# Attention maxima as three bfloat16 parts for a bfloat16 selector product, in a four-layer cross-attention kernel

## What is computed

```python
scores = jnp.einsum('bshd,bmhd->bhsm', qh, kh) / jnp.sqrt(hd)
probs = jax.nn.softmax(scores, axis=-1)
mem_out = jnp.einsum('bhsm,bmhd->bshd', probs, vh).reshape(B, S, D) @ Awo + abo
```

## Time and profile before

| what | us |
|---|---|
| median of three runs | 1187.8 (1187.23 to 1188.69) |
| time of the profiled execution | 1181.47 |
| its span, first to last instruction | 1179.7 |
| TensorE busy (matmul) | 981.0, 83% of the span |
| VectorE busy | 596.5, 51% |
| ScalarE busy | 428.1, 36% |
| mean granted TensorE clock | 0.873 of full |

### The profile page before, as it was taken

One profiled execution on the slowest core, in us unless ns is written; L12 is line 12 of the kernel. 1 busy time (PEld: TensorE's weight loads), 2 busy tenths in 40 slices (PEclk: granted clock), 3 DMA queues, 4 the chain that ended last, 5 costly groups with the idle time before them and its releaser, 6 DMA issues.

```text
span 1179.7 us, 11621 instructions
## 1 busy us (share of the span) xinstructions
PE 981.0 (83%) x4601; PEld 453.8 (38%) x4604; DVE 596.5 (51%) x881; ACT 428.1 (36%) x557; POOL 43.3 (4%) x42
## 2 busy tenths in 40 slices
PE   4867799669899899677799899895888798886877
PEld 2323244243344234253221443632346444542332
DVE  3238999972203210636821423516849774964342
ACT  3442222334322432363133143345572166123534
POOL 0000000200000000200000000000002000100000
PEclk9988899868998989776588789698989898987999
DMA  7000000000000000200000000000000000000000
GB/s 304 1 0 0 0 1 0 0 1 1 0 1 1 1 1 0 101 0 12 4 0 1 1 1 1 2 1 1 13 1 1 1 0 1 1 1 0 1 36 36
DMA packets 3526, 15.49 MB, mean 13 GB/s; under 512 B 933, under 2 KB 1445, under 8 KB 2842
## 3 DMA queue, kind: packets, MB, share of 16 engines
q1 hardware_dynamic: 3338, 12.77, 2.9%
q0 software_dynamic: 144, 2.10, 0.4%
HBM read 11.92 MB, written 2.10 MB: 12 GB/s over the span
## 4 chain that ended last, share of the span: by engine, by line
PE 57%; DVE 23%; ACT 9%; issue 8%; DMA 1%; SPq 1%; DVEq 0%; POOLq 0%; POOL 0%; ACTq 0%
PE ps L362 56%; DVE AR L1391 3%; DVE AR L1392 2%; ACT AR L572 2%; DVE AR L1544 2%; DVE AR L1689 1%; DVE VB L583 1%; DVE AR L461 1%; DVE AR L1394 1%; DVE AR L1676 1%; ACT AR L440 1%; DVE AR L1680 1%; DMA X<-in_xT 1%; DVE AR L1685 1%; ACT AR L445 1%
## 5 line engine op out<-in xcount | busy, mean ns | idle before, releaser
L362 PE MATMUL ps<-AR,WA 128*128 128x512 f32 (+3 forms) x808 | 365.8, 616 | 25.4 <-DVE AR L461 6.1
L362 PEld LDWEIGHTS ps<-AR,WA 128*128 128x128 f32 (+2 forms) x808 | 154.9, 197 | 230.6 <-issue 198.7
L362 PE MATMUL ps<-AR,CN 128*128 128x512 f32 (+3 forms) x350 | 147.1, 660 | 48.5 <-DVE AR L458 32.4
L362 PE MATMUL ps<-AR 128*64 128x128 f32 (+6 forms) x592 | 125.0, 373 | 11.1 <-DVE AR L1678 5.9
L362 PEld LDWEIGHTS ps<-AR,CN 128*128 128x128 f32 (+2 forms) x350 | 49.3, 175 | 116.0 <-issue 70.8
L591 DVE TENSOR_TENSOR AR<-ps,AR 128x512 f32<-128x512 f32 x24 | 16.6, 691 | 120.2 <-ACT AR L577 120.2
L583 DVE TENSOR_REDUCE VB<-ps 128x16 f32<-128x1232 f32 x32 | 45.3, 1440 | 46.2 <-PE ps L362 46.2
L362 PEld LDWEIGHTS ps<-AR 128*64 128x64 f32 (+5 forms) x592 | 49.8, 148 | 48.1 <-issue 22.9
L572 ACT ACTIVATE AR<-ps 77x2048 f32<-77x2048 f32 x24 | 44.1, 1870 | 61.4 <-PE ps L362 61.4
L1155 ACT ACTIVATE AR<-ps 128x512 f32<-128x512 f32 x48 | 28.7, 597 | 97.4 <-DVE AR L1394 49.9
L1468 DVE SCALAR_TENSOR_TENSOR X<-ps,VC,X 128x512 f32 x8 | 5.6, 747 | 106.7 <-PE ps L362 106.7
(11 more groups left out here) (271 smaller groups left out, 1133.9 us busy)
## 6 DMA issues: line engine op xcount, KB each, us to landing
WA<-in_m SPq DMA_DIRECT2D x1, 2856.0 KB, 9.1
WA<-in_m SPq DMA_DIRECT2D x1, 2560.0 KB, 14.3
X<-in_xT POOLq DMA_DIRECT2D x1, 2048.0 KB, 9.0
WA<-in_m SPq DMA_DIRECT2D x1, 2048.0 KB, 19.5
out<-X SPq DMA_DIRECT2D x4, 512.0 KB, 3.1
WB<-in_m SPq DMA_DIRECT2D x1, 1028.0 KB, 21.4
WA<-in_m SPq DMA_DIRECT2D x1, 512.0 KB, 15.1
VB<-AR SPq DMA_DIRECT2D x12, 32.0 KB, 1.8
```

What stands on the lines that cost most here:

```text
L362: return nc.tensor.matmul(out, lhsT, rhs, start=first, stop=last)
```

## The change

Each negated maximum m is written as three parts. `high` is m rounded to bfloat16, the remainder is formed in float32, rounded to bfloat16 again, and what is left is the third part. They lie in columns i, 4 + i and 8 + i of the head's 32 in `MXP[b]`, still a float32 tile, so that after the transposes they stand on three partitions. VectorE does this for each batch with six linked operations right after the batch's last maximum, 16 values for each set and partition at a time (32 in a0 and a3, 64 in a2), and counts up `att_ms`, for which the transposes of the batch now wait. The copy out of the accumulator writes `MXT[b]` in bfloat16. `sel` has ones in rows i, 4 + i and 8 + i, and is copied once, at the start, to the bfloat16 tile `SELB`. The selector product is one bfloat16 product for each head in place of a float32 one.

```diff
--- before.py
+++ after.py
@@ -84,7 +84,7 @@
         part = np.float32(np.trunc(rest / unit) * unit)
         c[k::32, CONST["neg"][0]] = part
         rest = np.float32(rest - part)
-    put("sel", p[:, None] % 32 == np.arange(4))
+    put("sel", (p[:, None] % 32 < 12) & (p[:, None] % 4 == np.arange(4)))
     put("half", (p[:, None] // 16 % 2 == np.arange(2)) * 16 ** -0.5)
     put("den", (p == 5)[:, None] * np.ones(6))
     put("head", p[:, None] % 32 == np.arange(HM))
@@ -253,7 +253,8 @@
         PF = [[a[:, 6 * T + k * ROWC * P:6 * T + (k + 1) * ROWC * P] for k in range(2)] for a in PX]
         PTX = [a[0:M, 0:8 * T].rearrange("m (s r t) -> m s r t", s=2, r=4) for a in PX]
         MXP = [VB[:, b * 1024:b * 1024 + T].rearrange("p (s n) -> p s n", s=SUB) for b in range(B)]
-        MXT = [VB[:, b * 1024 + T:b * 1024 + 2 * T] for b in range(B)]
+        MXT = [VB[:, b * 1024 + T:b * 1024 + T + T // 2].bitcast(BF16) for b in range(B)]
+        MXH = [VB[:, b * 1024 + T + T // 2:b * 1024 + T + T // 2 + 2 * SUB * 4].bitcast(BF16).rearrange("p (s r n) -> p s r n", s=SUB, r=4) for b in range(B)]
         PR = [[PF[b][k][:, 0:SLOTS * M].rearrange("p (h m) -> p h m", h=SLOTS) for k in range(2)] for b in range(B)]
         XC = [c3.take(DC, T) for _ in range(B)]
         RTB = [c3.take(T) for _ in range(B)]
@@ -333,6 +334,7 @@
         KEEP = sb("KEEP", [P, M])
         NEG3 = sb("NEG3", [P, HALF], BF16)
         ONESB = sb("ONESB", [P, P], BF16)
+        SELB = sb("SELB", [P, 4], BF16)
 
         class Chain:
 
@@ -531,7 +533,7 @@
                             last = mm(bank(b, r)[:, s * M:(s + 1) * M], QS[b][row, g, s * P:(s + 1) * P], KF[row, k, g, b, :], not masked, s == SUB - 1 or not masked)
                     last.then_inc(sem("att_p1"), 1)
             for b in BS:
-                pe.wait_ge(*after("att_mx", nset(p, j, len(sets) - 1, b)))
+                pe.wait_ge(*after("att_ms", nunit(p, j, b)))
                 for s in range(SUB):
                     last = nc.tensor.transpose(bank(b, 0)[:, s * P:(s + 1) * P], MXP[b][:, s, :], cn("ident"))
                 last.then_inc(sem("att_mt"), 1)
@@ -550,7 +552,7 @@
                             mm(bank(b, r)[0:M, :], KF[row, k, g, b, :], QS[b][row, g, :], True, False)
                         for r in range(4):
                             row = slice(32 * r, 32 * r + 32)
-                            last = mm(bank(b, r)[0:M, :], cn("sel")[row, i:i + 1].broadcast_to([32, M]), MXT[b][row, :], False, True)
+                            last = mm(bank(b, r)[0:M, :], SELB[row, i:i + 1].broadcast_to([32, M]), MXT[b][row, :], False, True)
                         last.then_inc(sem("att_p2"), 1)
                 for b in BS:
                     pe.wait_ge(*after("att_ex", nset(p, j, sets.index((g, PARTS[p] - 1)), b)))
@@ -576,12 +578,25 @@
                     act.wait_ge(*after("att_ln", nchunk(p, j, g, b)))
                     nc.scalar.activation(RTB[b], RTB[b], ACT.Exp, scale=-1.0).then_inc(sem("att_r"), 1)
 
-        def attn_dve(dve, p, j):
+        def attn_dve(dve, ch, p, j):
             for i, (g, k) in enumerate(key_sets(p)):
                 for b in BS:
                     dve.wait_ge(*after("att_p1", nset(p, j, i, b)))
                     nc.vector.tensor_reduce(MXP[b].rearrange("p s (r n) -> p r s n", n=32)[:, :, :, i],
                                             ps[:, 4 * b:4 * b + 4, 0:HALF].rearrange("p r (s m) -> p r s m", m=M), AX.X, ALU.max, negate=True).then_inc(sem("att_mx"), 1)
+                    if i < DC * PARTS[p] - 1:
+                        continue
+                    sets = DC * PARTS[p]
+                    parts = [MXP[b].rearrange("p s (r n) -> p s r n", n=32)[:, :, :, 4 * k:4 * k + sets] for k in range(3)]
+                    high = MXH[b][:, :, :, 0:sets]
+                    dve.wait_ge(*after("att_mx", nset(p, j, i, b)))
+                    for k in range(2):
+                        ch.link(nc.vector.tensor_copy(high, parts[k]))
+                        ch.link(nc.vector.tensor_tensor(parts[k + 1], parts[k], high, ALU.subtract))
+                        ins = nc.vector.tensor_copy(parts[k], high)
+                        if k == 0:
+                            ch.link(ins)
+                    ins.then_inc(sem("att_ms"), 1)
             for b in BS:
                 dve.wait_ge(*after("att_mt", nunit(p, j, b)))
                 nc.vector.tensor_copy(MXT[b], bank(b, 0)).then_inc(sem("att_mc"), 1)
@@ -1336,6 +1351,7 @@
             dve.wait_ge(*after("ld_vec", 16))
             dve.wait_ge(*after("ld_x", 16))
             dve.wait_ge(*after("ld_cn", 16))
+            nc.vector.tensor_copy(SELB[:, :], cn("sel"))
             norm_dve(dve, "r1", 0, lambda q: X[:, :, part_of(q)[0], part_of(q)[1]], RTR1, lambda q: XN[:, :, part_of(q)[0], part_of(q)[1]], False, None, SQR1,
                      UNITS, lambda q, k: ps[:, q, :])
             dve.wait_ge(*after("ld_w0", 16))
@@ -1450,7 +1466,7 @@
             dve.wait_ge(*after("mz", 1))
             with dve.Fori(0, J) as j:
                 ch.enter(j)
-                attn_dve(dve, "a0", j)
+                attn_dve(dve, ch, "a0", j)
                 for b in BS:
                     for mo in range(DC):
                         xd = X[:, mo, b, tj(j)]
@@ -1597,7 +1613,7 @@
             dve.wait_ge(*after("mz", 2))
             with dve.Fori(0, J) as j:
                 ch.enter(j)
-                attn_dve(dve, "a2", j)
+                attn_dve(dve, ch, "a2", j)
                 for b in BS:
                     for mo in range(DC):
                         xd = X[:, mo, b, tj(j)]
@@ -1703,7 +1719,7 @@
             with dve.Fori(0, J) as j:
                 ch.enter(j)
                 norm_dve(dve, "l3", j, lambda b: xs(b, j), RTB, lambda b: XC[b], True, XC, ST)
-                attn_dve(dve, "a3", j)
+                attn_dve(dve, ch, "a3", j)
                 for b in BS:
                     for mo in range(DC):
                         xd = X[:, mo, b, tj(j)]
```

## The result

| what | before | after |
|---|---|---|
| median of the runs, us | 1184.16 (20 runs beside it, 1181.91 to 1189.83) | 1191.65 (20 runs, 1186.67 to 1199.70) |
| ratio to before, 95% interval | | 1.0059 (1.0042 to 1.0077) |
| span of the profiled execution, us | 1179.7 | 1186.9 |
| mean granted TensorE clock | 0.873 | 0.859 |

A forecast was written before the change was run, and what follows sets the result against it. A sequence of handovers, no full engine, bounds the kernel (TensorE 57% of the chain, VectorE 23%). Delays of 16.7 us less savings gave +5.7, with layer 3's clock +6.7, on the median 1187.8: 1194.5 us, range 1190 to 1199.

The forecast's parts named there:

- the clock of layer 3: Layer 3: clock may fall before the second scores, costing 1.6 us a unit; a third taken, 0.5 each.
- Split, 1.36 and 1.56 us: Six linked VectorE operations per batch ahead of its transposes: 1.36 us in layers 0 and 3, 1.56 in layer 2.
- Delay of the second scores, 16.7: Second scores start two splits later: 2.56 us twice (layer 0), 2.96 twice (layer 2), 2.82 twice (layer 3).
- First product: A unit's first selector product (batch 0) counts whole: gains 1.54, 1.30, 1.40, 0.79 us, and 0.67 in layer 3.
- What ScalarE hides: Batch 1's first product is hidden behind batch 0's exponential, ScalarE taking 1.87 us a batch; not every saving counts.
- the second chunk's: In every unit's second chunk, one product between a batch's att_ctx and its exponential is on the path: 0.67 us gained.
- the small slacks: Waits of ScalarE that faster products remove: 0.27 us in the first unit, 0.29 in layer 2's second half.
- third rival: Clock falls in both layer 3 units and rises later in layers 0 and 2: +12.5, 1200.3 us; chance 0.19.
- A (-7.4): Selector's full saving lands in all 32 pairs of second scores: 24.1 us against 16.7 of delay, 1180.4; chance 0.08.
- B (no change): Clock has risen when layers 0 and 2's later second scores start: +1.3, 1189.1 us, no measurable change; chance 0.11.
- D (+15): The bfloat16 selector products run in turn, no faster than float32 ones: some +15, 1203 us; chance 0.04.
- the signs named beforehand: Profile after: 128 bfloat16 selector records, splits 1.3 to 1.6 us, back-to-back exponentials, half clock in layer 3's first scores.

The follow-up runs named there:

- e2: Changed kernel without the split: each maximum rounded to one bfloat16 part, bfloat16 selector product kept; ratio to before 0.9910.
- e3: Changed kernel with six more linked operations of the same shapes ahead of each split, into a spare tile; ratio to before 1.0233.
- e1: Changed kernel with the split kept but the selector product and its copy back in float32; ratio to before 1.0198.
- e4: Changed kernel with unread mask products (9 and 14) on TensorE while layer 3's splits run; ratio to before 1.0022.
- e7: Changed kernel with unread dense 512-column bfloat16 products on TensorE during the splits of all six units; ratio to before 0.9987.
- e5: Changed kernel with batch 0's split moved to GpSimd, VectorE splitting batch 1 only; ratio to before 0.9982.
- e6: Changed kernel with one bfloat16 part and no split in layers 0 and 2, layer 3 in float32 as before; ratio to before 0.9946.
- e8: Changed kernel with batch 0's split on GpSimd and 14 unread mask products ahead of batch 0's transposes in layer 3; ratio to before 0.9942.

## Why the prediction was right

Its mechanism was right, and its total; one term, the clock of layer 3, was mis-sized. Forecast +6.7 us with a range of 0.7 to 12.2 above the median; measured +7.0. The time itself, forecast at 1194.5, came out 2.9 lower, because the median of three runs that it starts from (1187.8) stood 3.6 above that of 20. By its own steps:

- **Split, 1.36 and 1.56 us.** Measured 1.29 (265.16 to 266.45) and, in layer 2, 690.32 - 688.92 = 1.40. The operations were at 0.18 and 0.19 us for 32 columns and 0.20 and 0.22 for 64. The slope taken from 8 and 512 columns held for the subtraction; the casts grew by less, and no cost of the strided layout shows.
- **Delay of the second scores, 16.7.** Measured 15.9: 2.44 and 2.19 in layer 0 (for 2.56), 2.52 twice in layer 2 (for 2.96), 3.12 in layer 3 (for 2.82). Layer 3's excess is 0.45 of transposes at half clock, which the text had counted under the clock. The 2.19 of the second unit holds the 0.47 us by which the first scores of the kernel before were slower; against e2's D it is 2.66. e3 confirms the sum from the other side.
- **First product.** Forecast gains of 1.54, 1.30, 1.40, 0.79; measured, in E, 1.46, 1.08, 1.18, 0.57. The new length is 2.47 at half clock and not 2.25: the next product starts 0.43 us after the selector products, as computed, but the exponential needs the end of the last one, whose record ends at 0.65. The columns gave the pitch, not the end. In the first unit the clock rose meanwhile, so that it took 2.32.
- **What ScalarE hides.** Only the first product, the second chunk's and the small slacks count. In layer 3 e2 gives -1.34 for 2 x 0.67. Summed over the units the terms make 11.2, less 0.2 in the first unit: 11.0. e2 shows 6.1 + 5.0 = 11.1 where the product stands, and e1 against the kernel after 12.6, of which 1.3 is layer 3's clock: 11.3. The rest of a unit after E gave back 0.73, 0.29, 0.95, 1.21, 0.67, 0.66, against the forecast 0.74, 0.67, 0.96, 0.96, 0.67, 0.67. Two things are hidden in this. Layer 2 has one slack more than the text counted: in the second chunk ScalarE waited 0.30 us for the last of four exponentials, which now runs back to back with those before it. So its rest falls by 1.21 where the clock is full, and not by 0.96. Last exponential of the first unit of layer 2 before, and the last three of it after:

```profile
710.29 1.87 ACT L572 ACTIVATE AR<-ps 77x2048 f32<-77x2048 f32 x1 [0.30 <-PE ps L362]
...
710.13 5.40 ACT L574 ACTIVATE AR<-ps 77x2048 f32<-77x2048 f32 x3 [0.30 <-PE ps L364]
```

And in the second and third unit the clock rises later than before: the key products of batch 1 run at half clock (1.93 us; 1.03 in the kernel before), which costs 0.67 - 0.29 = 0.38 and 1.21 - 0.95 = 0.26. In the second unit ScalarE waits 0.26 us between two exponentials that ran back to back. From the timeline of the kernel after:

```profile
385.53 1.93 PE L364 MATMUL ps<-AR,KF 32*77 32x512 f32 x8
...
387.93 1.87 ACT L574 ACTIVATE AR<-ps 77x2048 f32<-77x2048 f32 x1 [0.26 <-PE ps L364]
...
693.63 1.93 PE L364 MATMUL ps<-AR,KF 32*77 32x512 f32 x8
```

- **The clock in layer 3, the term that was mis-sized.** The mechanism and the price were right: 0.5 for the transposes and 1.1 for the first product, 1.6 a unit, and e4 measures 0.45 + 1.12 = 1.57. But "I take a third of it" was wrong: it fell ahead of the second scores in both units, 3.1 us and not 1.0. That part of the third rival came true. Its other part, the later rise in layers 0 and 2, is there in two units of four, for 0.38 and 0.26 us instead of 0.89.
- **The sum.** Without the clock of layer 3 the units stand at +4.9 (forecast 5.7), with it at +8.0 (forecast 6.7). The two errors, 0.8 too much net delay and 2.1 too little clock, have opposite signs, and about 1 us is then missing between the units' +8.0 and the +7.0 of the medians. The forecast is closer than its steps.
- **A rule and a trace.** By the Trainium skill (TensorE: Matmul & The Clock Gate, Part 1), throttling returns with an idle stretch. Read strictly, the transposes between the two splits would have kept the clock up. The trace does not agree: with 0.66 us of transposes in 4.10 us the clock fell.
- **The rivals.** A (-7.4) is refuted by e2 and e1. B (no change) did not occur, and e7 shows what it would have needed. D (+15) took four products in turn for 0.88 us; they end 0.39 us after their start at full clock, and the next product starts after 0.21.

Of the signs named beforehand these were seen: 128 bfloat16 records, six operations of 0.18 to 0.23 us, and batch 1's last maximum without idle time. Two failed in part. Exponentials are back to back in the first unit (x2 in one row of 3.64), not in the second. And no first scores of layer 3 ran at half clock (1.00 from 1099.00 to 1102.80): it fell behind them, between the two groups of transposes.

## What to carry to other kernels

Price a cheaper product only where nothing hides it: here 35.6 us of busy time held 11, because an exponential of 1.87 us stood over most of it. Small linked operations in the program of the engine that everything waits for cost their full length each time (1.3 us for six), and the clock that the waiting engine loses comes on top (1.57 us a unit in layer 3); give them to an idle engine (e5) or ask whether the exactness they buy is needed at all, since a softmax's subtracted maximum cancels (e6, outside the masked layer). Where a wait can't be avoided, some unread products in it can pay for themselves (e4, e8).

## What the runs showed of the hardware

- A busy TensorE was not always at full clock. In e7, TensorE was 92% busy with float32 products of 77 columns and 32 rows at clock 0.50 from 259 to 267; with seven products of 512 columns and 128 rows in the gaps of the next 4 us it rose to full, and the key products from 2.0 to 1.10 us. The profile's busy share and the granted clock have to be read side by side.
- GpSimd ran a small cast in 0.21 us and a subtraction of 32 columns in 0.25, against 0.18 and 0.19 on VectorE, 1.71 against 1.29 us for the chain of six. For operations this small it did as a second VectorE here.
- Four bfloat16 selector products of 512 columns on four row groups run side by side: 0.21 us to the next product at full clock, 0.39 to 0.40 to the end of their record; at half clock 0.43 and 0.65. What reads the result waits for the second figure.
